# A decoder block on one core: another order of the head, loads queued at once, and work moved between VectorE, ScalarE and GpSimd

## The reference

```python
def block(x, ctx):                     # x (4, 256, 256), ctx (4, 256, 64), all float32
    h = layernorm(x)                                   # 1
    q, k, v = heads(h @ Wq.T + bq), heads(h @ Wk.T + bk), heads(h @ Wv.T + bv)   # 16 heads of 16
    qp, kp = elu(q) + 1, elu(k) + 1
    attn = (qp @ (kp.T @ v)) / (qp . kp.sum(tokens) + 1e-6)          # linear attention
    x = x + merge(attn) @ Wo.T + bo
    s = (ctx @ Wxq.T + bxq) @ (ctx @ Wxk.T + bxk).T / 8              # scores (256, 256), 4 batches
    p = softmax(where(mask_ss | mask_key, -inf, s * layernorm(x)))   # 2
    x = x + p
    z = hadamard(layernorm(x) * SU_ug) / 64                          # 3
    z = silu(z @ Wgate.T * (s_gate * 64)) * (z @ Wup.T * (s_up * 64))  # 1024 wide
    z = hadamard(z * SU_dp) / 64
    return x + z @ Wdown.T * (Wscale_dp * 64)
```

## Time and profile before

| | |
|---|---|
| device time, median of 3 runs | 142.5 us (141.39 to 144.39) |
| the profiled execution: time, span | 142.54 us, 140.7 us |
| PE busy in it | 128.4 us, 91% of the span |
| DVE, ACT, GpSimd busy | 87.7, 74.7, 75.7 us |
| mean granted clock of TensorE | 0.976 |

### The profile page before, as it was taken

The page is one execution under the profiler, slowest core; times in us unless marked ns, Lnnn a source line. Parts: engine busy times, 40 slices in busy tenths (PEclk is TensorE's granted clock), DMA queues, the critical chain, the costliest instruction groups (busy, mean ns, idle before and its releaser), DMA issues.

```text
span 140.7 us, 2652 instructions
## 1 busy us (share of the span) xinstructions
PE 128.4 (91%) x995; PEld 121.7 (86%) x995; DVE 87.7 (62%) x213; ACT 74.7 (53%) x155; POOL 75.7 (54%) x82
## 2 busy tenths in 40 slices
PE   6868999798699999967899999999999999999991
PEld 2237989697699999966799999999999999999990
DVE  0489258999996799659897587676463440324202
ACT  0544378569359536493780857456738650155500
POOL 4291299699989879749384024455025432044610
PEclk9996589999999999999999999999999999999999
DMA  3999993000000000000000011000020000200002
GB/s 70 283 211 339 394 387 110 0 0 0 2 5 2 0 0 5 2 0 0 0 5 0 0 37 38 5 2 0 5 75 0 0 2 5 75 0 0 5 0 75
DMA packets 4817, 7.52 MB, mean 53 GB/s; under 512 B 576, under 2 KB 2944, under 8 KB 4676
## 3 DMA queue, kind: packets, MB, share of 16 engines
q1 hardware_dynamic: 4496, 7.02, 15.8%
q10 hardware_dynamic: 308, 0.32, 0.8%
HBM read 6.29 MB, written 1.05 MB: 52 GB/s over the span
## 4 chain that ended last, share of the span: by engine, by line
PE 64%; DVE 21%; issue 5%; ACT 4%; DMA 3%; POOL 1%; POOLq 0%
PE bank L1077 27%; PE bank L1090 16%; PE bank L982 6%; PE bank L954 3%; PE bank L1041 3%; DVE st L615 3%; DMA x_res<-in_x 3%; PE bank L1003 2%; PE bank L1063 2%; DVE xT L777 2%; DVE xn L631 1%; PE bank L986 1%; DVE wo L652 1%; PE bank L1023 1%; DVE at L708 1%
## 5 line engine op out<-in xcount | busy, mean ns | idle before, releaser
L1077 PE MATMUL bank<-xh_home,wug 128*128 128x256 f32 x384 | 49.3, 284 | 0.0
L1077 PEld LDWEIGHTS bank<-xh_home,wug 128*128 128x128 f32 x384 | 47.2, 191 | 0.2
L302 POOL TENSOR_TENSOR hs<-front,hs 128x256 fp32r<-128x256 f32 x32 | 25.1, 790 | 32.1 <-ACT hs L509 32.0
L500 ACT ACTIVATE front<-bank,vecs 128x256 f32<-128x256 f32 x32 | 15.2, 474 | 22.3 <-PE bank L1077 22.1
L792 DVE SCALAR_TENSOR_TENSOR front<-bank,sc_up,front 128x256 f32<-128x256 f32 x32 | 15.3, 480 | 18.4 <-ACT front L500 18.4
L1090 PE MATMUL bank<-wdh,hs 128*128 128x256 f32 x192 | 23.8, 283 | 0.0
L1090 PEld LDWEIGHTS bank<-wdh,hs 128*128 128x128 f32 x192 | 23.4, 191 | 0.0
L252 POOL TENSOR_TENSOR rstd<-veps,mhalf 128x2 f32<-128x2 f32 x12 | 8.6, 715 | 22.7 <-DVE veps L620 22.4
L982 PE MATMUL bank<-wqkv,xT 128*128 128x256 f32 x96 | 16.5, 314 | 2.6 <-DVE xT L668 1.8
L982 PEld LDWEIGHTS bank<-wqkv,xT 128*128 128x128 f32 x96 | 14.5, 215 | 3.1 <-DVE xT L668 2.0
L509 ACT CAST hs<-front 128x256 fp32r<-128x256 f32 x32 | 12.8, 400 | 4.5 <-DVE front L792 4.4
(11 more groups left out here) (105 smaller groups left out, 217.6 us busy)
## 6 DMA issues: line engine op xcount, KB each, us to landing
wd_a<-in_w_d SPq DMA_DIRECT2D x1, 1024.0 KB, 7.7
front<-in_w_ug SPq DMA_DIRECT2D x2, 512.0 KB, 7.5
back<-in_w_ug SPq DMA_DIRECT2D x2, 512.0 KB, 8.7
out<-x_res SPq DMA_DIRECT2D x8, 128.0 KB, 2.0
wd_b<-in_w_qkv SPq DMA_DIRECT2D x3, 256.0 KB, 5.8
x_res<-in_x SPq DMA_DIRECT2D x2, 256.0 KB, 4.8
x_res<-in_x SPq DMA_DIRECT2D x1, 512.0 KB, 7.1
back<-in_ctx_t ACTq DMA_DIRECT2D x1, 260.0 KB
```

The source lines that it names most:

```text
L302: g.tensor_tensor(hs[:, 1, n % JB, :], sg[:, n % RING, :], hs[:, 0, n % JB, :].bitcast(F32), ALU.subtract)\
L500: a.activation(sg[:, n % RING, :], B("GU", n)[:, 0:SEQ], ACT.Silu, scale=vecs[:, V_WSUG + JB + j:V_WSUG + JB + j + 1]).then_inc(s["sg"], 1)
L1077: ins = mm(dst[:, n * SEQ:(n + 1) * SEQ], wug[:, wa, k, at_col + j * P:at_col + (j + 1) * P], xh[b][:, xb, k, :], start=(i == 0), stop=(i ...
```

## The change

- Warm-up: 19 matmuls on zeros at the start and 3 behind T1 of batch 0, for 8 and 11 behind mx. `HEAD` begins with T1 and K; mx, u and SC come later; T1 of batch 2 and OUT move relative to the products of the other batches; SC of batch 1 comes last but four. In batch 0 the groups of `SIDE` come one or two products earlier (XH of batch 1 is no longer inside `down`).
- Loads: SP waits for nothing but the SBUF of the last two quarters of w_up and w_gate. Tile 0 of x is loaded by SP, tile 1 by ScalarE's queue, then w_k, w_v and w_q, whose lines are now contiguous in 2 KB; the context goes to SP's queue behind x of tiles 2 and 3; w_down comes behind the masks, constants and w_o, and its row of scales last. `wo_raw` has SBUF of its own.
- Biases are split in two: the 256 of K first, the 512 of V and Q later. `bias_lo` of K stands ahead of `normalise1(0)` on DVE, and `bias_hi` of K and the row of ones first on ScalarE.
- Epsilon is added by GpSimd in `rstd_of`; the mean is negated by ScalarE (`negate_mean`); high parts of the context and the masks' floats are made by ScalarE; GpSimd waits for both halves of the bias before the low part of the context; `sc_up` (128x8) is made by DVE.
- `scale_pre` is gone; `add_y` multiplies each result by the scale in PSUM before it adds it. Butterflies are issued in halves with other work between.
- Scores of batch 1 are written to `probs` once softmax of batch 0 has been added (`x2` is 2), and are not copied.
- Transposes wait for each tile and go tile by tile.

```diff
-WARM, WARM_MORE = 8, 11
+WARM, WARM_MORE = 19, 3
-HEAD = (("mx", 0), ("T1", 0), ("K", 0), ("V", 0), ("u", 0), ("Q", 0), ("u", 1), ("T1", 1), ("ST", 0), ("SC", 0),
-        ("K", 1), ("NUM", 0), ("V", 1), ("AT", 0), ("Q", 1), ("SC", 1), ("OUT", 0), ("T1", 2), ("ST", 1), ("K", 2),
-        ("SC", 2), ("NUM", 1), ("V", 2), ("SC", 3), ("T1", 3), ("Q", 2), ("AT", 1), ("T3", 0), ("K", 3), ("OUT", 1),
+HEAD = (("T1", 0), ("K", 0), ("mx", 0), ("V", 0), ("Q", 0), ("u", 0), ("T1", 1), ("ST", 0), ("u", 1), ("K", 1),
+        ("SC", 0), ("NUM", 0), ("V", 1), ("AT", 0), ("T1", 2), ("Q", 1), ("OUT", 0), ("ST", 1), ("K", 2), ("NUM", 1),
+        ("V", 2), ("SC", 2), ("AT", 1), ("Q", 2), ("T1", 3), ("OUT", 1), ("SC", 3), ("T3", 0), ("K", 3), ("SC", 1),
         ("XH", 0), ("V", 3), ("Q", 3), ("ST", 2))
-SIDE = {(0, 0): (("ST", 3),), (0, 2): (("NUM", 2),), (0, 4): (("WD", 0), ("WD", 1)), (0, 5): (("AT", 2), ("WD", 2), ("WD", 3)),
-        (0, 6): (("T3", 1),), (0, 7): (("OUT", 2),), (0, 8): (("XH", 1),),
+SIDE = {(0, 0): (("ST", 3),), (0, 1): (("NUM", 2),), (0, 2): (("T3", 1),), (0, 3): (("WD", 0), ("WD", 1)),
+        (0, 4): (("AT", 2), ("WD", 2), ("WD", 3)), (0, 5): (("XH", 1),), (0, 7): (("OUT", 2),),
...
@block.sync
+            sp.dma_start(xs[:, 0:1, :], x[:, 0:1, :]).then_inc(ld["x0"], 16)
+            sp.dma_start(qkv_raw[:, 0], w_qkv[:, 0]).then_inc(ld["wk"], 16)
+            sp.dma_start(qkv_raw[:, 1], w_qkv[:, 1]).then_inc(ld["wv"], 16)
+            sp.dma_start(qkv_raw[:, 2], w_qkv[:, 2]).then_inc(ld["wq"], 16)
+            sp.dma_start(xs[:, 2:4, :], x[:, 2:4, :]).then_inc(ld["x2"], 16)
+            sp.dma_start(ctxT, ctx_t).then_inc(ld["ctx"], 16)
+            sp.dma_start(xs[:, 4:8, :], x[:, 4:8, :]).then_inc(ld["x3"], 16)
...
@block.gpsimd
             def rstd_of(n, b):
+                pool.wait_ge(s[f"aggr{n}"], 2 * b + 2)
+                g.tensor_scalar(veps[:, n - 1, two], mv[:, n - 1, two, 1], LN_EPS, 1.0, ALU.add, ALU.mult).then_inc(s[f"eps{n}"], 1)
...
             rstd_of(1, 0)
-            ctx_parts(0)
-            ctx_parts(1)
+            pool.wait_ge(s["bias"], 2)
+            ctx_lo(0)
             rstd_of(1, 1)
             shift_of(1, 1)
-            mask_bias()
-            pool.wait_ge(ld["row"], 16)
-            add_ob(0)
+            ctx_lo(1)
             rstd_of(1, 2)
             shift_of(1, 2)
-            pool.wait_ge(s["pre_scaled"], 2)
-            butterfly(0)
+            mask_sum()
+            add_ob(0)
+            butterfly(0, 0)
...
@block.scalar
-            act.dma_start(wx[:, :], w_x).then_inc(ld["wx"], 16)
-            act.dma_start(ctxT, ctx_t).then_inc(ld["ctx"], 16)
+            act.dma_start(xs[:, 1:2, :], x[:, 1:2, :]).then_inc(ld["x1"], 16)
+            act.dma_start(cst[:, 0:P], const[:, 0:P]).then_inc(ld["ident"], 16)
             act.wait_ge(s["bias_zero"], 1)
             act.dma_start(bias_raw[ROW_HI:BIAS_ROWS:ROW_LO, :], bias).then_inc(ld["bias"], 16)
+            act.dma_start(wx[:, :], w_x).then_inc(ld["wx"], 16)
...
+            bias_hi(K_COLS)
+            one_rows()
+            w_hi("wk", 0)
+            xT_hi(0)
+            w_hi("wv", 1)
+            w_hi("wq", 2)
+            bias_hi(VQ_COLS)
+            ctx_hi(0)
+            exp_k(0)
             mx_hi()
             v_copy(0)
+            negate_mean(1, 1)
+            ctx_hi(1)
             normalise(1, 1, xn)
             exp_q(0)
+            negate_mean(1, 2)
+            xT_hi(1)
+            u_hi(0)
+            normalise(1, 2, xn)
             u_hi(1)
+            wo_hi()
+            exp_k(1)
+            mask_bias()
+            negate_mean(1, 3)
             ug_hi(0)
...
@block.vector
+            ln_stats(1, 0)
+            bias_lo(0, K_COLS)
+            normalise1(0)
+            w_lo(0)
+            xT_lo(0)
...
             elu_q(0)
             xT_lo(1)
-            u_lo(1)
             dve.wait_ge(ld["cst"], 16)
             diagonal(0)
-            scale_pre(1)
-            ln1_stats(2)
-            elu_k(1)
-            attend(0)
-            wo_lo()
+            u_lo(0)
+            u_lo(1)
+            wo_lo()
+            ln_stats(1, 3)
+            scale_up()
+            attend(0)
+            elu_k(1)
             at_lo(0)
...
             def add_y(b):
+                if b == 0:
+                    dve.wait_ge(ld["wsd"], 16)
                 for i in range(ST):
                     t = ST * b + i
                     wait_full(dve, "Y", b, i)
-                    v.tensor_tensor(xs[:, t, :], B("Y", b, i)[:, 0:HID], xs[:, t, :], ALU.add).then_inc(read_of("Y", b, i), 1)
+                    y = B("Y", b, i)[:, 0:HID]
+                    v.tensor_tensor(y, y, rows[:, 1, :], ALU.mult).then_inc(s["y"], 1)
+                    dve.wait_ge(s["y"], t + 1)
+                    v.tensor_tensor(xs[:, t, :], y, xs[:, t, :], ALU.add).then_inc(read_of("Y", b, i), 1)
...
@block.tensor
             def scores(b):
                 wait_read(pe, "u", b // 2)
-                dst = take("SC", b)
+                if b == 1:
+                    pe.wait_ge(s["x2"], 2)
+                dst = B("SC", b) if b < ST else take("SC", b)
             def turn(name, b, src):
                 dst = take(name, b)
-                for f in range(FB):
-                    for i in range(ST):
+                for i in range(ST):
+                    if name != "AT":
+                        pe.wait_ge(s["xn" + name[1]], ST * b + i + 1)
+                    for f in range(FB):
...
             def turn1(b):
...
+                if b == 0:
+                    warm(WARM_MORE)
```

More of the change, by code:

```diff
@@ L81, in schedule @@
         order += [g for j in (JB, JB + 1) for name, i in SIDE.get((b, j), ()) for g in banks_of(name, i)]
-    order.remove(("SC", 0, 0))
-    return order
+    return [g for g in order if g not in (("SC", 0, 0), ("SC", 1, 0))]
 def decoder_kernel(nc, x, ctx_t, w_qkv, bias, w_o, w_x, w_ug, w_d, vec, row, mask_ss, mask_key, const, out):
@@ L195, in wait_read @@
             eng.wait_ge(read[bank_of[name, i, t]], turn_of[name, i, t] + 1)
-        loads = "x0 x1 x2 ident cst wk wv wq ctx wx bias vec row mss mkey wo wd ug0 ug1 ug2 ug3".split()
+        loads = "x0 x1 x2 x3 ident cst wk wv wq ctx wx bias vec ob wsd mss mkey wo wd ug0 ug1 ug2 ug3".split()
         ld = {n: sem("ld_" + n) for n in loads}
@@ L370, in _, with one_rows, negate_mean, ctx_hi @@
             a.activation(exp_first[:, :], mhalf[:, :], ACT.Exp)
-            a.mul(ones[:, :], neg1[0:BIAS_ROWS, :].to_broadcast([BIAS_ROWS, HID]), -1.0).then_inc(s["ones"], 1)
+            def one_rows():
+                a.mul(ones[:, :], neg1[0:BIAS_ROWS, :].to_broadcast([BIAS_ROWS, HID]), -1.0).then_inc(s["ones"], 1)
+            def negate_mean(n, b):
+                two = slice(2 * b, 2 * b + 2)
+                act.wait_ge(s[f"aggr{n}"], 2 * b + 2)
+                a.mul(nmean[:, n - 1, two], mv[:, n - 1, two, 0], -1.0).then_inc(s[f"nmean{n}"], 1)
+            def ctx_hi(c):
+                cols = slice(c * 512, (c + 1) * 512)
+                act.wait_ge(ld["ctx"], 16)
+                a.copy(ctxr[:, 0, cols], ctxT[:, cols]).then_inc(s["ctx_hi"], 1)
+            def mask_bias():
+                act.wait_ge(s["msum"], 2)
+                a.mul(mbias[:, :, :].rearrange("p t s -> p (t s)"), bytes_of[:, 0:TILES * SEQ], MASKED).then_inc(s["mbias"], 1)
             def mx_hi():
@@ L586, in _ @@
             prob(3)
+            negate_mean(3, 3)
             for n in range(2 * JB, 3 * JB):
@@ L764, in xh_lo, with scale_up @@
                     .then_inc(read_of("XH", b), 1)
-            def scale_pre(n):
-                part = slice(n * JB // 2, (n + 1) * JB // 2)
-                if n == 0:
-                    dve.wait_ge(ld["row"], 16)
-                    dve.wait_ge(ld["wd"], 16)
-                v.tensor_tensor(wd_a[:, part, :], wd_a[:, part, :], rows[:, 1:2, :].to_broadcast([P, JB // 2, HID]),
-                                ALU.mult).then_inc(s["pre_scaled"], 1)
+            def scale_up():
+                dve.wait_ge(ld["vec"], 16)
+                v.tensor_tensor(sc_up[:, :], vecs[:, V_WSUG:V_WSUG + JB], vecs[:, V_SUD:V_SUD + JB], ALU.mult).then_inc(s["sc_up"], 1)
             def pre_lo(n):
```

241 lines of the change are left out of this document (105 added, 136 removed).

## The result

| | before | changed |
|---|---|---|
| device time, median | 142.54 us (4 runs, 141.39 to 144.39) | 137.50 us (4 runs, 137.41 to 137.59) |
| profiled execution: time, span | 142.54, 140.7 us | 137.59, 135.8 us |
| PE, DVE, ACT, GpSimd busy | 128.4, 87.7, 74.7, 75.7 us | 126.4, 80.2, 78.2, 71.3 us |

The ratio is 0.967, 95% interval 0.962 to 0.973: faster by 3.3%. The forecast was 137.0.

A forecast was written before the change was run, and what follows sets the result against it. The prediction saw a chain of about 10 us up to the first K, then PE's work, as the bound. Its sum was 142.54 - 1.1 - 3.2 - 2.1 + 0.9 = 137.0 us, range 133.6 to 140.6.

The forecast's parts named there:

- the start: Up to K of batch 0: K at 9.2 us, 1.1 us earlier, held by the bias; bounds 0 and 2.1.
- the clock: PE from 11.78 to 18.20 us: with the new zeros the clock stays up, saving 3.2 us; bounds 0 and 3.2.
- idle time in the head and batch 0: PE from the start of K of batch 0 on: 3.9 us idle instead of 6.0, 2.1 us less.
- the end: Last two `add_y` multiplications are not hidden: 0.9 us later; bounds 0.4 and 1.1.
- What bounds the kernel: A chain of about 10 us up to the first K, then PE's work, with 9.2 us that could go.
- Queues up to AT: Lists up to AT of batch 0: DVE is later than PE, so AT starts at 24.1 instead of 28.17 us.
- After that: Behind AT of batch 0: DVE and GpSimd relieved, ScalarE some 4 us more, only small PE gaps left.
- The rest: PE's later work stays the same and dense; six of eight `add_y` multiplications, about 0.42 us each, are hidden.
- late loads: Rival: loads queued at once share bandwidth with w_k, K starts at 13.7 and the clock falls: 144.7 us; 6 in 100.
- the relief does nothing: Rival: gaps only move, DVE's list stays the limit or ScalarE replaces it: 139.1 to 140.9 us; 16 in 100.
- The clock falls anyway: Rival: PE still idles around the first K and before AT, so the clock falls, price 3.2: 140.2 us; 10 in 100.
- Faster than forecast: Rival: the bias comes early and the gaps close: 134.0 us; 14 in 100.

The follow-up runs named there:

- e_norm_first: The changed kernel with `normalise1` of batch 0 ahead of `bias_lo` of K on DVE: 137.08 us.
- n_best: The changed kernel with `scale_up` behind the low part of T1 of batch 2, `normalise1` before `bias_lo`, and third-norm means of batches 1 to 3 negated later: 134.30 us.
- e_eps_dve: The changed kernel with epsilon added by DVE behind the statistics again, negated means staying on ScalarE: 139.41 us.
- b_mul_late: The kernel before with `scale_pre` taken out and the scales multiplied onto the result in PSUM in `add_y`: 140.61 us, ratio 0.982.
- e_no_mul: The changed kernel with the multiplication by w_down's scales in `add_y` left out altogether: 136.18 us.
- e_sp_waits: The changed kernel with SP waiting for w_k before queueing x of tiles 2 and 3, and for w_q before x of tiles 4 to 7: 137.25 us.
- b_warm19: The kernel before with 19 matmuls on zeros at the start and 3 behind T1, instead of 8 and 11: 142.37 us, ratio 1.001.
- e_warm8: The changed kernel with 8 instead of 19 matmuls on zeros at the start, the 3 behind T1 kept: 138.43 us.
- n_wds: n_best with w_down's scales applied by DVE to the four WD products in PSUM instead of to the eight results: 133.72 us, ratio 0.948.

## Why the prediction was right, point by point

Its sum, against the two profiled executions. The start is K's, 10.32 to 9.75. The next two terms lie between it and the end of `down` of batch 0 and are PE's busy time there, 64.13 to 61.47 us, and its idle time, 6.01 to 2.52. Then come the time from there to the first result, and the end.

| term | forecast | measured |
|---|---|---|
| the start | -1.1 | -0.6 |
| the clock (PE's busy time) | -3.2 | -2.7 |
| idle time in the head and batch 0 | -2.1 | -3.5 |
| batches 1 to 3 | 0 | +1.0 |
| the end | +0.9 | +0.9 |
| sum | -5.5 | -4.9 (time 4.95) |

So the sum is closer than its terms. Idle time fell by 1.4 more than forecast, and the start, the clock and batches 1 to 3 were forecast too well by 0.5, 0.5 and 1.0: that these nearly balance is luck. Part of the 0.5 of the clock is mx, 0.33 us, which stood ahead of K before and stands behind it now.

*What bounds the kernel*: right. A dense PE behind the head passes on what the head gains; 1.25 us taken from one wait of PE came out whole at the last `down`.

*The start*: the bias was the limit as forecast, within 0.2 us. The term was too large by half a microsecond: `normalise1` started at 7.84, not 7.6, and T1 took another 0.49 behind its end, where I had counted 0.3; the rest is handoffs. What holding it behind `bias_lo` costs was 0.3 to 0.4 (e_norm_first). A step beside the path was wrong too: x in two halves landed at 5.14, though I called 4.70 an upper bound, and rstd was ready at 7.26 instead of 6.6. With the bias hidden the gain could not have been 2.1.

*The clock*: right for the executions compared, and half right as a price. I took the fall of the traced execution for the kernel's property. It is there in most runs but not in all, and the runs without it are 1.6 us faster in the median than those at 0.976, not 3.2. That the profiled execution was of the most frequent kind (11 of 27), and the median too, is luck. "19 in a row last to about 7.5, wherever in them the clock rises" was wrong: they ended between 7.0 and 8.5, and in n_best T1 waited for them.

*Queues up to AT*: forecast 24.1, measured 24.90 with a wait of 1.41 (forecast 1.7). Two sizes in it were wrong and nearly cancelled each other: `wo_lo` took 0.94 instead of 2.0, and `scale_up` 1.49 instead of 0.2. The other 0.7 is the start of `u_lo(1)`, 19.62 instead of 18.9. The rule that DVE with two SBUF inputs and GpSimd exclude each other (the Trainium skill, SBUF — State Buffer, Who interferes with whom) covers both, and the trace agrees: `wo_lo` started at 20.23, ahead of the butterfly at 20.58, which then took 2.85 us instead of 2.4, and `scale_up` at 21.97, inside it, and paid. What the forecast lacked was which comes first. The 128x2 epsilon in e_eps_dve, with one input in SBUF, was held alike (1.35 and 1.51), and that rule, of two inputs, doesn't name it.

*After that*: GpSimd was done at 55.4 and not at 53, its last subtraction took 3.40 us instead of 2.40; no wait of PE shows it. That ScalarE's wait in `negate_mean(1, 3)` costs nothing held. I looked for this danger there and missed it at `negate_mean(3, 1)` to `(3, 3)`; the last two keep the table load back. The 0.6 before the fifth `gate_up` didn't come, 0.7 instead of 0.4 before T3 of batch 1 and 0.4 before T1 of batch 3 did. Which part closed the waits before K of batch 2 (1.8) and before WD (1.4) no run isolates; `scale_pre` alone didn't, since b_mul_late still has 1.6 and 1.4 there.

*The rest*: here a step failed. "Six are hidden under PE's dense stretch" is true of PE's products but not of the transposes that wait for DVE and ScalarE: two delays, 0.96 us in all. The second, 0.5, goes with the multiplications (e_no_mul), and both with the means negated later (n_best). So the second needs both causes, and the first hangs on the late means or on something else that n_best moved; that wasn't taken apart.

*Rivals*: late loads at the price of several microseconds are out; w_k was no limit. But the conclusion that the bias can't be slower for what is queued behind it doesn't hold for ScalarE's queue (e_sp_waits): it is worth up to 0.4. That the relief does nothing is out. "The clock falls anyway" happened in b_warm19, in e_warm8 and in one run of e_eps_dve, there behind a wait of 1.85 us, and not in the changed kernel, though PE waits 1.4 us before AT. Faster than forecast is what n_best and n_wds are.

## What to carry to other kernels

In front of a dense engine, at full clock, the only costs are its waits, and each is found by reading the neighbour's list just ahead of what it waits for: there one instruction on 128x8 numbers was worth 1.25 us, and an edit that took 2.8 us of work out of the same list 0.7, less than it gave back at the end. When a wait is moved to another engine, look at what that engine would have done meanwhile, a table load too. And price a clock fall from several runs with their clocks, not from the one that was traced.

## What the runs showed of the hardware

Matmuls on zeros took different times from run to run, eleven of them 2.55, 2.94 and 4.38 us and nineteen 5.70 to 7.17: how many of them run at 0.45 us and how many at 0.23 isn't set by the program alone, and the granted clock of the profile, 1.00 over all of them, doesn't tell. Whether it fell later in the kernel before differed from run to run too, at a mean clock from 0.964 to 1.00. PE's wait of 1.8 us before K of batch 2 was followed by a fall in b_warm19 and by none in the kernel before. An instruction of 0.15 us took 1.49 beside a GpSimd instruction of 2.85, and with epsilon ahead of it epsilon took 1.35 and it took 0.15: one small DVE instruction pays, the first to come. And with SP's later loads held back the 13 KB of vectors on ScalarE's queue landed 3.9 us after issue instead of 7.6.
